# Gathers, sums and additions of batch 1's experts moved into the block of the recurrent stage, beside the first unit (batch 0)

## The reference, cut to what matters

```python
# layer 0, after attention: 64 experts, 6 per token
topk_w, topk_i = lax.top_k(masked_scores, K)            # K = 6
topk_w = topk_w / (topk_w.sum(axis=-1, keepdims=True) + 1e-08)
h = silu(einsum('th,eih->eti', x, eg_w)) * einsum('th,eih->eti', x, eu_w)
routed = einsum('eti,ehi,te->th', h, ed_w, comb)        # the weighted sum over a token's 6 experts
# layer 1: modulated layer norm of the sum, then the recurrent network
# per layer and token: layernorm, time mixing of k, v, r;
ww = u + kk; qq = maximum(pp, ww)
e1 = exp(pp - qq); e2 = exp(ww - qq)
out = (e1 * aa + e2 * vv) / (e1 * bb + e2)
qq2 = maximum(pp + w, kk)
aa, bb = e1b * aa + e2b * vv, e1b * bb + e2b
```

## Time and profile before

| what | us |
| --- | --- |
| three timed executions: lowest, median, highest | 1044.67, 1053.04, 1057.72 |
| the profiled execution: its own time | 1046.67 |
| span in the profile, first to last instruction | 1045.0 |
| busy in the span: PE, DVE, ACT, POOL | 869.2, 724.9, 565.3, 253.7 |
| mean granted TensorE clock | 0.912 of full speed |

### The profile page before, as it was taken

How to read it: one execution, slowest core, us unless ns; L and a number is a source line. 1 busy time by engine, 2 the same in 40 slices (tenths; PEclk the granted TensorE clock), 3 DMA queues, 4 the chain that set the end, 5 groups by cost and what they waited for, 6 DMA issues and landing times. The chain is left out here.

```text
span 1045.0 us, 13432 instructions
## 1 busy us (share of the span) xinstructions
PE 869.2 (83%) x4333; PEld 448.6 (43%) x4333; DVE 724.9 (69%) x1323; ACT 565.3 (54%) x888; POOL 253.7 (24%) x348
## 2 busy tenths in 40 slices
PE   6899999999885439998996006789999999998998
PEld 3553443444222219887886002333433443343433
DVE  4879888888476616655663234679988988997575
ACT  4324666666762105554553003649768877875743
POOL 1011222222115777714751771000000000000000
PEclk9899999999986579999998557879999999998999
DMA  3732565542012126746772112000000010000001
GB/s 88 236 79 45 190 198 172 160 144 70 23 53 93 51 87 216 229 158 200 225 222 92 52 51 73 0 0 9 2 23 11 7 46 1 0 1 0 1 0 41
DMA packets 51054, 87.48 MB, mean 84 GB/s; under 512 B 11202, under 2 KB 22832, under 8 KB 49200
## 3 DMA queue, kind: packets, MB, share of 16 engines
q1 hardware_dynamic: 36716, 58.56, 18.8%
q10 hardware_dynamic: 8128, 15.47, 4.0%
q0 software_dynamic: 6144, 12.60, 3.9%
HBM read 43.28 MB, written 40.89 MB: 81 GB/s over the span
## 5 line engine op out<-in xcount | busy, mean ns | idle before, releaser
L1066 ACT ACTIVATE pt<-psum 128x1024 f32<-128x1024 f32 (+1 forms) x192 | 149.9, 814 | 111.5 <-PE psum L808 111.1
L1218 DVE TENSOR_REDUCE part_max<-psum 128x1 f32<-128x512 f32 (+3 forms) x304 | 184.3, 658 | 31.6 <-PE psum L790 19.1
L786 PE MATMUL psum<-ka,qa 72*128 72x512 bf16 (+3 forms) x384 | 113.7, 337 | 5.4 <-DVE part_max L1218 2.0
L746 POOL DMA_INDIRECT part<-slot_y,slot_row x96 | 92.9, 968 | 86.5 <-DMA slot_y<-pt 57.8
L735 POOL DMA_INDIRECT slot_x<-va,slot_row x96 | 96.3, 1004 | 36.4 <-issue 29.0
L725 POOL TENSOR_SCALAR_AFFINE_SELECT pt<-pt 128x256 f32<-128x256 f32 x128 | 52.3, 410 | 215.4 <-ACT pt L1066 214.8
L808 PE MATMUL psum<-qa,ka 75*128 75x512 bf16 (+3 forms) x384 | 94.5, 328 | 3.0 <-ACT pt L1066 1.4
L824 PE MATMUL psum<-pt,va_g 128*32 128x512 f32 (+3 forms) x768 | 82.7, 503 | 0.5 <-POOL pt L725 0.3
L1426 DVE TENSOR_TENSOR moe_hid<-moe_silu,psum 128x256 f32<-128x256 f32 x56 | 23.4, 418 | 84.6 <-ACT moe_silu L1186 78.8
L110 ACT ACTIVATE ln_sq<-psum 128x512 f32<-128x512 f32 x44 | 26.1, 594 | 98.4 <-PE psum L93 98.3
L786 PEld LDWEIGHTS psum<-ka,qa 72*128 72x128 bf16 x384 | 37.1, 98 | 79.4 <-DVE part_max L1218 60.0
(11 more groups left out here) (316 smaller groups left out, 1650.3 us busy)
## 6 DMA issues: line engine op xcount, KB each, us to landing
slot_x<-zero ACTq DMA_DIRECT2D x8, 1792.0 KB, 7.0
pt<-slot_x SPq DMA_DIRECT2D x56, 256.0 KB, 3.4
slot_y<-pt SPq DMA_DIRECT2D x56, 256.0 KB, 2.0
...
```

The lines of the kernel that those rows point to most:

```text
L746: pool.indirect_dma_start(out=yg[:, n % 4, j, :], out_offset=None, in_=ys_d[b], in_offset=bass.IndirectOffsetOnAxis(ap=row[:, n, j:j + 1], ...
L786: mm = pe.matmul(bank[:, nk * h:nk * (h + 1)], qa[0:ROWS, g % RING, h0 + h, chunk(i, P)], ka[0:ROWS, g % RING, h0 + h, k0:k0 + nk], start= ...
L1066: act.activation(pt[:, u % 4, :, 0:n], score_bank[u % 2][:, :, 0:n], ACT.Exp, scale=SCALE)\
L1218: dve.tensor_reduce(part_max[:, h0:h0 + heads, slot], bank_of("fill", f)[:, 0:heads * nk].rearrange("p (h n) -> p h n", h=heads), AX_X, AL ...
```

## The change

POOL's gathers of batch 1 stand at the head of its list in `stage_rwkv`, ahead of the constants `expand` that only the last stage uses. The first block ends when chunks 0 and 1 of x are complete. The eight `combine` steps of batch 1 are spread over DVE's list in the recurrent stage: one behind the entry of batch 0, one behind the time norm, one behind `addend`, one behind `scans`, four behind `fractions(0)`. Then come the two additions and the whole entry of batch 1 (`enter_mod`, `enter_ln0`), which stood between the steps of unit 0 before. PE and ACT have the entry of batch 1 behind unit 0's matmuls and sigmoid. The squares and reciprocal roots of `enter_mod` lie in the tile `relu`, which unit 0 doesn't use yet, instead of `gap` and `n2`. The functions keep their instructions; nothing is added or removed but one wait (`mod_centre` for `x_l0`).

```diff
--- before.py
+++ after.py
@@ stage_core @@
-        row = m.sb("slot_row", [P, NT, 8], I32)
+        row = G.row
-        weight = m.sb("slot_weight", [P, NT, TOP])
+        weight = G.weight
...
-        comb_bank = [G.bank[0], G.bank[4], G.bank[1], G.bank[5]]
+        comb_bank = [G.bank[0], G.bank[4]]
...
@@ stage_core, gpsimd @@
-                for b in range(B):
-                    gather(b)
+                gather(pool, G, 0)
@@ stage_core, tensor @@
-                for c in range(NC):
-                    turn_combined(c)
+                for c in range(2):
+                    turn_combined(pe, G, c, comb_bank[c])
@@ stage_core, vector @@
-                    for n in range(BLOCKS, NT):
-                        combine(n)
-                    for c in range(NC):
-                        add_experts(c)
+                    for c in range(2):
+                        add_combined(dve, G, c, comb_bank[c])
@@ new functions beside the stages; their bodies stood inside stage_core before @@
+def gather(pool, G, b):
+
+    for r in range(4):
+        pool.wait_ge(G.ys_out[r], 16 * (G.sets // 4) * (b + 1))
+    for n in range(8 * b, 8 * b + 8):
+        if n >= 4:
+            pool.wait_ge(G.combined, n - 3)
+        for j in range(6):
+            pool.indirect_dma_start(out=G.yg[:, n % 4, j, :], out_offset=None, in_=G.ys_d[b],
+                                    in_offset=bass.IndirectOffsetOnAxis(ap=G.row[:, n, j:j + 1], axis=0))\
+                .then_inc(G.gathered[n % 4], 16)
+def combine(dve, G, n):
+
+    r = n % 4
+    dve.wait_ge(G.scattered[n // 8], 16 * G.indexed)
+    dve.wait_ge(G.gathered[r], 16 * 6 * (n // 4 + 1))
+    dve.tensor_tensor(G.yg[:, r, :, :], G.yg[:, r, :, :], G.weight[:, n, :].unsqueeze(2).to_broadcast([P, 6, P]), ALU.mult)\
+        .then_inc(G.weighted, 1)
+    dve.wait_ge(G.weighted, n + 1)
+    dve.tensor_reduce(G.h_tok[:, n, :], G.yg[:, r, :, :].rearrange("p j m -> p m j"), AX_X, ALU.add).then_inc(G.combined, 1)
+def turn_combined(pe, G, c, bank):
+    pe.wait_ge(G.combined, 4 * c + 4)
+    for t in range(4):
+        mm = pe.transpose(bank[:, chunk(t, P)], G.h_tok[:, 4 * c + t, :], G.ident[:, :])
+    mm.then_inc(G.comb_psum, 1)
+def add_combined(dve, G, c, bank):
+    dve.wait_ge(G.comb_psum, c + 1)
+    dve.scalar_tensor_tensor(G.x[:, chunk(c)], bank[:, :], G.mod[:, 0, 5, c // 2:c // 2 + 1],
+                             G.x[:, chunk(c)], ALU.mult, ALU.add).then_inc(G.x_l0, 1)
@@ stage_rwkv @@
-        mod_sq = [gap[:, chunk(q)] for q in range(2)]
-        mod_rs = [n2[:, chunk(q)] for q in range(2)]
+        mod_sq = [rl[:, q, :] for q in range(2)]
+        mod_rs = [rl[:, 2 + q, :] for q in range(2)]
@@ stage_rwkv, gpsimd @@
+                gather(pool, G, 1)
                 pool.memset(expand[:, :, :, :], 0.0).then_inc(expand_done, 1)
@@ stage_rwkv, tensor @@
                 def mod_centre(q):
+                    pe.wait_ge(G.x_l0, 3 + q)
...
-                mod_centre(0)
-                mod_centre(1)
                 in_centre(0)
                 in_centre(1)
-                mod_var(0)
                 ln_variance(pe, G, ln_in(0), 0)
                 ln_variance(pe, G, ln_in(1), 1)
-                mod_var(1)
...
-                pe.wait_ge(G.h_in, 3)
                 keys(0, 0)
-                pe.wait_ge(G.h_in, 4)
                 keys(0, 1)
+                values(0, 0)
+                values(0, 1)
+                receptance(0, 0)
+                receptance(0, 1)
+                pe.wait_ge(v_kept, 2)
+                pe.wait_ge(sig_done, 1)
+                for q in range(2):
+                    turn_combined(pe, G, 2 + q, G.bank[6 + q])
+                mod_centre(0)
+                mod_centre(1)
+                mod_var(0)
+                mod_var(1)
                 in_centre(2)
                 in_centre(3)
-                values(0, 0)
-                values(0, 1)
                 ln_variance(pe, G, ln_in(2), 0)
                 ln_variance(pe, G, ln_in(3), 1)
-                receptance(0, 0)
-                receptance(0, 1)
@@ stage_rwkv, scalar: mod_square and mod_rstds, and square, log, rstd of ln_in(2) and ln_in(3) @@
...
+                sigmoids(0)
+                mod_square(0)
+                mod_square(1)
+                mod_rstds(0)
+                mod_rstds(1)
+                square(ln_in(2), 0)
+                square(ln_in(3), 1)
...
@@ stage_rwkv, vector @@
-                enter_mod(0)
-                enter_mod(1)
+                combine(dve, G, 8)
                 time_scale(0, 0)
                 time_bias(0, 0)
                 time_scale(0, 1)
                 time_bias(0, 1)
+                combine(dve, G, 9)
                 peak(0)
...
                 addend(0)
+                combine(dve, G, 10)
                 scans(0)
+                combine(dve, G, 11)
+                fractions(0)
+                for n in range(12, NT):
+                    combine(dve, G, n)
+                for q in range(2):
+                    add_combined(dve, G, 2 + q, G.bank[6 + q])
+                enter_mod(0)
+                enter_mod(1)
                 for q in range(2):
                     enter_ln0(dve, G, ln_in(2 + q), 2 + q, r_new)
-                fractions(0)
@@ build: part, va, slot_row and slot_weight are allocated outside the attention scope, so that they outlive it @@
+        G.part = mem.sb("part", [P, 2, 3, 2, CH], BF16)
+        G.va = mem.sb("va", [P, NG, 8, HG * DK])
+        G.row = mem.sb("slot_row", [P, NT, 8], I32)
+        G.weight = mem.sb("slot_weight", [P, NT, 6])
...
```

45 lines of the change are left out of this document (6 added, 39 removed).

## The result

| | before | after |
| --- | --- | --- |
| median of the runs, us | 1050.41 (1044.67 to 1057.72, 4 runs) | 1022.8 (1017.68 to 1039.0, 4 runs) |
| ratio | | 0.9746, 95% interval 0.97 to 0.9792 |
| the profiled execution, us | 1046.67 | 1025.12 |
| its span, us | 1045.0 | 1023.4 |
| mean granted TensorE clock | 0.912 | 0.928 |

The change makes the kernel faster by 2.1 to 3.0%. The run of 1039.0 us fell in the chip's slower state and is left out of the ratio. Run again later: 1025.43 against 1048.76 of the kernel before (five and nine runs), ratio 0.9763, interval 0.9699 to 0.9827: faster again, though this interval alone doesn't exclude a gain of less than 2%.

A forecast was written before the change was run, and what follows sets the result against it. The bound was 68 us set by GpSimd's gathers of batch 1, uncovered by layer 1's work. From the profiled 1046.7, less 22.8 saved, came 1023.9; half of 6.4 added for the median gave 1027 us, range 1013 to 1041.

The forecast's parts named there:

- Part 1: Start of layer 1: comes at 568.9, 68.2 us earlier than before; batch 1's gathers start at 569.2 instead of 568.90.
- Part 2: Unit 0 beside the gathers: VectorE done with it at about 620, combines 12 to 14 at 627; GpSimd still last.
- D: Later units: the gain is taken back as units 1 and 2 catch up with hidden work; 1044 to 1053, chance 0.06.
- Part 3: Batch 1's gathers on GpSimd: VectorE's operations hold their starts, adding 8.3 us to the 60.0 of the 48 gathers.
- The zero for tensor_scalar: Unit 0 on VectorE: its tensor_scalar operations, about 7 us in all, cost the gathers nothing.
- rival C: Gathers beside unit 0: series hold as a whole, or tensor_scalar holds too; hold 12 to 19, 1031 to 1038, chance 0.20.
- Part 4: Exposed tail behind the last gather: unit 0's output comes at 665.6 instead of 688.36, saving 22.8 us.
- 9.8 us to `rw`, the same now: End of the tail: from the start of `body(1)` to unit 0's output takes 9.8 us as before, at granted clock 0.61.
- A: Gathers beside unit 0: holds as costed, 6 to 11 us; saved 20 to 25, 1025 to 1030, chance 0.50.
- the clock's 3 us: Last 9.8 us of the tail: 3 us less if TensorE's clock stayed at its upper level there.
- B: Gathers beside unit 0: they keep their pace, hold 0 to 4 us; saved 27 to 31, 1019 to 1023, chance 0.20.
- E: Gathers and unit 0: VectorE and GpSimd hold each other, 2.2 us per gather; slower than before, 1067, chance 0.04.

The follow-up runs named there:

- the order alone: The changed kernel with batch 1's gathers and combines back at the end of the first block, everything else as in the change: 1061.84 us, ratio 1.0147.
- the changed kernel with TensorE busy: The changed kernel with 112 unused small matmuls on TensorE in its waits ahead of the last transposes: 1025.13 us, ratio 0.9735.
- the output early and TensorE busy: The changed kernel with unit 0's last steps ahead of the last combines, and 68 unused small matmuls in TensorE's wait: 1015.76 us, ratio 0.9683.

## Why the prediction was right

The forecast was 1027 us in a range from 1013 to 1041, the measurement 1022.8, and the reason given holds: the gathers stay what ends last, and unit 0 now runs beside them. By distances from the first gather, where forecast and traces can be compared:

| step | forecast | measured |
| --- | --- | --- |
| first gather, against the one before's | 0.3 later | about 0 (the common start is 5.0 later, the gather 5.04) |
| hold over 48 gathers | 8.3 | 7.25 |
| last gather's end to sum's end | 4.0 | 4.46 |
| sum's end to the modulated norm's bias | 8.3 | 7.6 |
| entry norm | 6.0 | 6.0 |
| from there to `rw` | 9.8 | 7.5 |
| first gather to `rw` | 96.4 (before: 119.46) | 92.8 |
| saved | 22.8 | 26.7 |

**Part 1 held.** Only the 0.3 us for the barrier and the five waits was too much. Of the signs that I had named, the gathers' mean is 1.102 us (above 1.1), and the last gather's end and the first norm of unit 1, at 641.18 and 659.23, are 636.1 and 654.2 less the common 5.0, where I had 637 or 638 and 656.

**Part 2 held in what the time rests on, and its times were wrong.** GpSimd was the last to come, as forecast. I had VectorE done with unit 0 at about 620, and it was at 618.9, but that is a coincidence of the later start: behind the first gather it is 45.0 us where I had 50.8. `peak` came 22.6 us behind the first gather instead of 27.9, because I had moved its old time by 68.2 and forgotten that batch 1's entry norms, which stood ahead of it, were gone. From the first matmul of layer 1 to `peak` it is 28.2 us before, 24.9 with the order alone, where the first norm still starts at the lower clock (3.66 us for four matmuls), and 23.8 now (1.95). The error changed nothing in the time, since VectorE then only waited: 1.28 us at combine 12, and 5 us at each of the next three. What lay in the cover cost nothing either: `rw` to the end of the span is 356.7 us, before 356.6. That also settles D: nothing was given back later.

**Part 3 was right in size, with one wrong reading.** The forecast's 2.9 for scans was 3.2 (1.19, 1.11, 0.92), its 3.8 for unit 0's two-operand operations 2.2 (0.15, 1.02, 1.02), its 1.6 for the combines' multiplies 1.4 (0.67, 0.75). The zero for tensor_scalar was wrong: 0.45 in four gathers (0.08, 0.18, 0.11, 0.08). The earlier trace rows had not shown that it doesn't hold, but that a VectorE operation which starts behind the DMA doesn't; in the earlier trace rows and in every hold since, the operation had started at least 0.06 us ahead of the DMA. Two that started 0.01 and 0.02 ahead in the profile of after (at 617.62 and 627.64) held nothing. The same explains the eight multiplies of the earlier trace rows that held none: the profile of after has one at 620.16, 0.03 us behind the start of the gather at 620.13, which took 0.95. In rival C the combination "tensor_scalar holds" was true and its 12 to 19 us false, because the hold ends with the single operation.

The Trainium skill's SBUF — State Buffer, section "Who interferes with whom", says that in a two-port mode, which tensor_scalar can enter, VectorE and GpSimd exclude each other for the whole instruction, and that the second to come waits. The trace agrees in part. The gather at 584.06, second to a tensor_scalar, waited. The other way round VectorE waited little or not at all: the biases at 589.85 and 591.15, begun 0.6 us behind a gather's start, took 0.61 and 0.57 us instead of 0.49, and those at 577.97 and 579.15, begun 0.2 to 0.3 behind one, kept their 0.49, as did both sides in the earlier trace rows. A gather thus doesn't keep VectorE out for its whole 0.95 us. What I had drawn from the section, a hold of 11 us, was wrong: the operations are short beside the gathers' 1.25 us, and few gathers meet one.

**Part 4 is the term that was mis-sized.** The step "9.8 us to `rw`, the same now" failed: it took 7.5. Before, this norm ran at a granted clock of 0.61 with four matmul instructions in 3.78 us; now it was 0.95 over the norm (0.82 over the whole tail), and the same four took 2.36. I had named the 3 us that the upper level would bring, and put the forecast in the middle. The modulated norm's 0.7 us are in part the same error: its bias was forecast 8.3 us behind the sum, and came after 7.6, its first four matmuls taking 3.06 us where I had counted on the 3.50 of the earlier trace rows. Why the clock held stays open. Before, TensorE had been idle for 3.62 us ahead of this norm, now for 1.79, with two norms of both chunks straight in front of it. Behind idle times of 3.62, 3.86, 4.08 and 5.36 us four such matmuls took 3.78. But a short idle time doesn't settle it: behind 1.79 us they took 2.36 in the change and 3.39 once with the order alone (at 652.45), and behind 1.89 us 2.36 in the changed kernel with TensorE busy and 3.65 with the output early and TensorE busy. The tail starts slow, as forecast (3.06 us for the first four, 1.98 where TensorE was kept busy).

**Against it** stood 0.46 us from the last gather to the sum's end; 0.23 of it is `expand`, which I had at nothing, since without it the distance is 4.23.

**The rivals.** A (6 to 11 us of hold) is the one that happened, with the clock's 3 us on top: saved are 26.7 us instead of A's 20 to 25. That the time of 1022.8 lies below A's 1025 to 1030 fits this, but proves little, since the repeat, at 1025.43, lies in it. B, though its 1019 to 1023 holds the number, is refuted: the hold was 7.25, not 0 to 4. E needed a pace of 1.9 us per gather; it was 1.4 (67.24 / 48).
